# Experts' gate scale from maxima, routing weights on GpSimd, and a shifted order in a shared-and-routed MLP kernel

## What is computed

```python
def _gemma_mlp(x, gate_w, up_w, down_w):
    g = jnp.einsum('bsh,hi->bsi', x, gate_w)
    u = jnp.einsum('bsh,hi->bsi', x, up_w)
    return jnp.einsum('bsi,ih->bsh', gelu(g) * u, down_w)

rw = softmax(router_logits); w, sel = top_k(rw, 2); w = w / w.sum(-1)
dense_w = zeros((B, E)).at[arange(B)[:, None], sel].add(w)
out = sum over e of dense_w[:, e] * _gemma_mlp(x, skill_gate[e], skill_up[e], skill_down[e])
x = x + out + _gemma_mlp(x, shared_gate, shared_up, shared_down)
```

## Time and profile before

| | |
|---|---|
| median of 3 runs | 211.62 us (211.42 to 211.68) |
| the profiled execution | 211.93 us, its span 210.1 us |
| TensorE busy (2695 matmuls) | 205.2 us |
| VectorE busy | 123.6 us |
| ScalarE busy | 133.8 us |
| GpSimd busy | 117.9 us |
| granted TensorE clock | 1.0 all through |
| loads from HBM | 9.18 MB, landed in the first 26 us |

### The profile page before, as it was taken

One profiled execution on the slowest core, in us unless ns is written; L12 is line 12 of the kernel. 1 busy time (PEld: TensorE's weight loads), 2 busy tenths in 40 slices (PEclk: granted clock), 3 DMA queues, 4 the chain that ended last, 5 costly groups with the idle time before them and its releaser, 6 DMA issues.

```text
span 210.1 us, 6672 instructions
## 1 busy us (share of the span) xinstructions
PE 205.2 (98%) x2695; PEld 165.0 (79%) x2695; DVE 123.6 (59%) x217; ACT 133.8 (64%) x217; POOL 117.9 (56%) x129
## 2 busy tenths in 40 slices
PE   7999999989999999999999999999999999999995
PEld 2444555445444478899999999999999999999995
DVE  2899657977999988554353444434435435344452
ACT  6283767677989997655656656556565565655650
POOL 3023644359548997665565655655656556565562
PEclk9999999999999999999999999999999999999999
DMA  6999600000000000000010010010010010010011
GB/s 196 391 433 434 296 2 0 0 3 0 2 0 5 0 0 3 0 3 5 3 53 3 0 53 3 3 53 0 3 55 3 3 53 0 3 53 4 3 50 53
DMA packets 2813, 11.70 MB, mean 56 GB/s; under 512 B 352, under 2 KB 608, under 8 KB 2400
## 3 DMA queue, kind: packets, MB, share of 16 engines
q1 hardware_dynamic: 2640, 11.01, 13.1%
q10 hardware_dynamic: 144, 0.26, 0.7%
HBM read 9.18 MB, written 2.10 MB: 54 GB/s over the span
## 4 chain that ended last, share of the span: by engine, by line
PE 93%; DVE 4%; issue 1%; ACT 0%; POOL 0%; POOLq 0%
PE o_ps L664 7%; PE g_ps L646 7%; PE u_ps L646 7%; PE o_ps L663 7%; PE u_ps L645 7%; PE g_ps L645 7%; PE u_ps L644 7%; PE g_ps L644 7%; PE o_ps L662 7%; PE u_ps L612 3%; PE g_ps L612 3%; PE g_ps L614 2%; PE o_ps L627 2%; PE o_ps L625 2%; PE o_ps L626 2%; PE g_ps L613 2%
## 5 line engine op out<-in xcount | busy, mean ns | idle before, releaser
L304 POOL TENSOR_TENSOR h<-h 128x512 f16<-128x512 f32 x92 | 109.2, 1194 | 79.2 <-ACT h L340 57.9
L457 DVE SCALAR_TENSOR_TENSOR h<-gel,sk_factor,u_ps 128x512 f32<-128x512 f32 x64 | 47.8, 747 | 68.0 <-PE u_ps L646 39.0
L335 ACT ACTIVATE gel<-g_ps,sk_gate 128x512 f32<-128x512 f32 x64 | 43.9, 687 | 49.8 <-PE g_ps L646 49.8
L340 ACT CAST h<-h 128x512 f16<-128x512 f32 x92 | 56.0, 609 | 3.5 <-DVE h L457 3.5
L645 PE MATMUL g_ps<-x,wsk 128*128 128x128 f16 x256 | 46.2, 219 | 0.0
L646 PE MATMUL g_ps<-x,wsk 128*128 128x128 f16 x256 | 46.2, 219 | 0.0
L645 PE MATMUL u_ps<-x,wsk 128*128 128x128 f16 x256 | 46.2, 219 | 0.0
L646 PE MATMUL u_ps<-x,wsk 128*128 128x128 f16 x256 | 46.2, 219 | 0.0
L644 PE MATMUL u_ps<-x,wsk 128*128 128x128 f16 x256 | 46.2, 219 | 0.0
L644 PE MATMUL g_ps<-x,wsk 128*128 128x128 f16 x256 | 46.2, 219 | 0.0
L663 PE MATMUL o_ps<-h,wsk 128*128 128x128 f16 x256 | 45.9, 219 | 0.0
(11 more groups left out here) (103 smaller groups left out, 310.1 us busy)
## 6 DMA issues: line engine op xcount, KB each, us to landing
wsk<-skills SPq DMA_DIRECT2D x3, 2048.0 KB, 16.1
outT<-xT SPq DMA_DIRECT2D x7, 256.0 KB, 2.0
xT<-xT SPq DMA_DIRECT2D x2, 768.0 KB, 6.3
wsh<-shared SPq DMA_DIRECT2D x3, 256.0 KB, 3.9
xT<-xT ACTq DMA_DIRECT2D x1, 256.0 KB, 3.5
xT<-xT SPq DMA_DIRECT2D x1, 256.0 KB, 4.6
outT<-xT SPq DMA_DIRECT2D x1, 192.0 KB, 2.6
outT<-xT SPq DMA_DIRECT2D x1, 64.0 KB, 1.5
```

What stands on the lines that cost most here:

```text
L304: nc.gpsimd.tensor_tensor(hidden_lo(t), hidden_full(t), hidden_hi(t), ALU.subtract).then_inc(lo_ok, 1)
L335: nc.scalar.activation(gel[:, t % NG, :], g_ps[t % 2][:, :], ACT.Gelu_apprx_tanh, scale=scale).then_inc(gelu_ok, 1)
L340: nc.scalar.copy(hidden_hi(t), hidden_full(t)).then_inc(hi_ok, 1)
L457: nc.vector.scalar_tensor_tensor(out=h32[:, t % N32, :], in0=gel[:, t % NG, :], scalar=factor, in1=u_ps[t % 2][:, :], op0=ALU.mult, op1=AL ...
```

## The change

Four things change.

The experts' gate weights get their scale as x does: VectorE reduces them in steps 5 to 8, 1024 columns each (`part_top`), `mask` reduces the four maxima to one and squares it, and TensorE sums the square. The gram of the gate is gone from TensorE; GRAMS holds the two that stay.

The routing weights and their spreading move from VectorE at step 3 to GpSimd, behind `shared_tables(FIRST)` and in front of its first subtraction; one fused operation becomes two. The reciprocal moves on VectorE to the end of `probabilities`.

The low half of the shared down weights and `x_low(0)` move from behind `hidden(4)` to in front of it.

The hand-written order shifts: K_UP's gram begins at step 9 instead of 10, K_DOWN's at 16 instead of 15; the masks stand at 8, 11, 14, 20 (K_GATE, X_REST, K_UP, K_DOWN) and their sums at 10, 14, 17, 23; before, at 9, 12, 14, 19 and 11, 14, 16, 21. The last three x groups are reduced one step earlier, their high halves come one step later, the experts' pieces one step earlier, the tables of the experts two steps later.

```diff
-        TOP_AT = {1: (2,), 3: (3, 4), 10: (5,), 11: (6,), 12: (7,)}
-        TOP_OF = {FIRST: 3 + XF, X_NEXT: 3 + XA, X_REST: 3 + G}
-        K_STEPS = [5, 10, 15]
-        MASK_AT = {3: X_NEXT, 9: K_GATE, 12: X_REST, 14: K_UP, 19: K_DOWN}
-        SPREAD_AT = {4: X_NEXT, 11: K_GATE, 14: X_REST, 16: K_UP, 21: K_DOWN}
+        TOP_AT = {1: (2,), 3: (3, 4), 9: (5,), 10: (6,), 11: (7,)}
+        TOP_OF = {FIRST: 3 + XF, X_NEXT: 3 + XA, X_REST: 4 + G, K_GATE: 4 + XA}
+        PART_AT = {5: (GATE, 0), 6: (GATE, 1), 7: (GATE, 2), 8: (GATE, 3)}
+        K_STEPS = {K_UP: 9, K_DOWN: 16}
+        MASK_AT = {3: X_NEXT, 8: K_GATE, 11: X_REST, 14: K_UP, 20: K_DOWN}
+        SPREAD_AT = {4: X_NEXT, 10: K_GATE, 14: X_REST, 17: K_UP, 23: K_DOWN}
         ROUTE_AT = 6
-        ROUTED_AT = 11
+        ROUTED_AT = 10
-        SKILL_TABLES_AT = 23
-        X_AT = {3: 0, 5: 2, 8: 3, 11: 4, 15: 5, 19: 6, 23: 7}
+        SKILL_TABLES_AT = 25
+        X_AT = {3: 0, 5: 2, 8: 3, 12: 4, 16: 5, 20: 6, 24: 7}
-        PIECES = {12 + 2 * n: n for n in range(3 * E // EG)}
+        PIECES = {11 + 2 * n: n for n in range(3 * E // EG)}
...
+            def routing_weights():        # on GpSimd
+                pool.wait_ge(r_step, 6)
+                nc.gpsimd.tensor_copy(route[:, TOP_K:], top_i[:, 0:TOP_K])
+                nc.gpsimd.tensor_scalar(w_raw[:, :], top_v[:, 0:TOP_K], rpair[:, 0:1], None, ALU.mult).then_inc(r_weight, 1)
+                pool.wait_ge(r_weight, 1)
+                nc.gpsimd.tensor_scalar(w_live[:, :], w_raw[:, :], 1.0 / NUM_MOE_LAYERS, None, ALU.mult)
+                nc.gpsimd.tensor_scalar(w_rest[:, :], w_raw[:, :], 1.0 - 1.0 / NUM_MOE_LAYERS, None, ALU.mult).then_inc(r_weight, 1)
+                pool.wait_ge(r_weight, 2)
+                nc.gpsimd.tensor_tensor(route[:, 0:TOP_K], w_rest[:, :], w_live[:, :], ALU.add).then_inc(r_weight, 1)
+                pool.wait_ge(r_weight, 3)
+                for q in range(2 * TOP_K):
+                    nc.gpsimd.tensor_scalar(spread[:, :, q], ident[0:B, 0:B], route[:, q:q + 1], None, ALU.mult).then_inc(r_spread, 1)
...
+            def part_top(kind, n):
+                if n == 0:
+                    dve.wait_ge(sk_in[kind], 16)
+                nc.vector.tensor_reduce(parts[:, n:n + 1], wsk32[:, (kind * E + 2 * n) * I:(kind * E + 2 * n + 2) * I],
+                                        AX.X, ALU.max, apply_absolute_value=True).then_inc(part_ok, 1)
...
-                if n not in K_OF:
+                if n in K_OF and n not in GRAMS:
+                    kind = K_OF.index(n)
+                    dve.wait_ge(part_ok, E // 2)
+                    tops(KC + kind, parts[:, :])
+                if n not in GRAMS:
...
             for t in range(STEPS):
+                if t == C:
+                    shared_low(DOWN, 3)
+                    x_low(0)
                 hidden(t)
-                if t - 1 in X_AT:
+                if t - 1 in X_AT and t != C:
                     x_low(X_AT[t - 1])
...
+                if t in PART_AT:
+                    part_top(*PART_AT[t])
...
-                if t == C:
-                    shared_low(DOWN, 3)
...
-                if t == C - 1:
-                    routing_weights()
-                    routing_spread()
```

More of the change, by code:

```diff
@@ L73, in build @@
         ident = sb("ident", [P, P], F32)
+        parts = sb("parts", [P, E // 2], F32)
         floor = sb("floor", [P, 3 + XF], BF16)
@@ L108, in build @@
         w_raw = sb("w_raw", [B, TOP_K], F32)
+        w_rest = sb("w_rest", [B, TOP_K], F32)
         w_live = sb("w_live", [B, TOP_K], F32)
@@ L136, in build @@
         r_step = sem("r_step")
+        r_weight = sem("r_weight")
         r_spread = sem("r_spread")
@@ L141, in build @@
         top_ok = sem("top_ok")
+        part_ok = sem("part_ok")
         gram_ok = sem("gram_ok")
@@ L174, in build @@
         K_OF = (K_GATE, K_UP, K_DOWN)
+        GRAMS = (K_UP, K_DOWN)
         COLS = [(DC, XC + XF), (XC + XF, XC + XA), (KC, KC + 1), (XC + XA, XC + G), (KC + 1, KC + 2), (KC + 2, KC + 3)]
@@ L294, in skill_tables @@
                                         wexp[:, :, :].rearrange("p (j r) k -> p j (r k)", r=GR), ALU.mult).then_inc(tab_sk, 1)
+            def routing_weights():
[10 more added lines that the diff above has]
+                    nc.gpsimd.tensor_scalar(spread[:, :, q], ident[0:B, 0:B], route[:, q:q + 1], None, ALU.mult).then_inc(r_spread, 1)
             shared_tables(FIRST)
+            routing_weights()
             for t in range(C, STEPS):
@@ L394, in mask @@
                 else:
-                    kind = K_OF.index(n)
-                    dve.wait_ge(gram_ok, kind + 1)
+                    dve.wait_ge(gram_ok, GRAMS.index(n) + 1)
                     nc.vector.scalar_tensor_tensor(out=diag[:, :], in0=n_ps[0][:, 0:P], scalar=NORM_FLOOR,
@@ L403, in scales @@
                 norm = n_ps[1][:, 0:b - a]
-                if n in K_OF:
+                if n in GRAMS:
                     norm = n_all[:, a:b]
                     nc.vector.tensor_reduce(norm, n_ps[1][:, 0:P], AX.X, ALU.max).then_inc(n_red, 1)
-                    dve.wait_ge(n_red, K_OF.index(n) + 1)
+                    dve.wait_ge(n_red, GRAMS.index(n) + 1)
                 nc.vector.tensor_scalar(e_bits[:, a:b], norm.bitcast(U32), 1, EXP_MASK,
@@ L487, in probabilities @@
                 nc.vector.tensor_tensor(pair[:, :], top_v[:, 0:1], top_v[:, 1:2], ALU.add).then_inc(r_step, 1)
-            def routing_weights():
                 dve.wait_ge(r_step, 5)
-                nc.vector.tensor_copy(route[:, TOP_K:], top_i[:, 0:TOP_K]).then_inc(r_step, 1)
                 nc.vector.reciprocal(rpair[:, :], pair[:, :]).then_inc(r_step, 1)
[L493 to L504, removed]
             def routed_tables():
@@ L698, in _ @@
                     down_first(1)
-                for kind in range(3):
-                    n = t - K_STEPS[kind]
+                for batch in GRAMS:
+                    kind = K_OF.index(batch)
+                    n = t - K_STEPS[batch]
                     if 0 <= n < 4:
@@ L703, in _ @@
                             pe.wait_ge(sk_in[kind], 16)
-                        if n == 0 and kind:
-                            pe.wait_ge(diag_ok, K_OF[kind - 1] + 1)
+                        if n == 0 and batch == K_DOWN:
+                            pe.wait_ge(diag_ok, K_UP + 1)
                         a = (kind * E + 2 * n) * I
                         for half in range(2):
-                            last = gram(n_ps[0][:, 0:P], wsk32[:, a + half * I:a + (half + 1) * I],
-                                        n == 0 and half == 0)
+                            last = gram(n_ps[0][:, 0:P], wsk32[:, a + half * I:a + (half + 1) * I], n == 0 and half == 0)
                         if n == 3:
```

## The result

The changed kernel takes 209.61 us (median; 209.51 to 209.69) against 211.65 of the kernel before run beside it: a ratio of 0.9907 with a 95% interval of 0.9884 to 0.9930, 2.04 us less. On another chip the ratio was 0.9920 (0.9892 to 0.9949). The forecast was 209.8 us.

A forecast was written before the change was run, and what follows sets the result against it. TensorE was taken as the bound, with VectorE deciding only where its masks are late. Terms -1.84 - 0.49 - 1.01 + 0.5 + 0.68 + 0.35 = -1.81 us gave 209.8 us from the 211.62 median, range 208.5 to 211.3.

The forecast's parts named there:

- The products, -1.84: Steps 5 to 8: TensorE loses a row of eight 128-column products each, 0.46 us per row, 1.84 us saved.
- X_REST's mask, -0.49: Step 14's sum: the mask, moved to step 11, comes in time, so TensorE's 0.49 us wait goes whole.
- VectorE as pace of steps 5 to 11, +0.68: VectorE without a gap from hidden(5) delays x_low(3), so TensorE waits 0.68 us by step 8's down products.
- Two low halves: Before hidden(4): they fill the routing's place; X_NEXT's scales then escape GpSimd's 0.8 us hold-up, with no gain yet.
- The lock between VectorE and GpSimd at steps 2 and 3, +0.5: GpSimd's small routing operations slip between VectorE's two-input operations, delaying the X_NEXT sum 0 to 0.85 us; 0.5 taken.
- Rival B: Freed time turns into waits: VectorE-GpSimd lock 0.85, K_UP's mask late 0.8, reductions at 1.25; 211.0 us, chance 0.24.
- K_UP's mask, -1.01 + 0.35: K_DOWN gram: the 1.01 us wait goes; an even chance of a 0.7 us wait for the mask adds 0.35.
- A: New waits don't come: the lock costs nothing, reductions take 1.05 us, K_UP's mask is in time; 208.6 us, chance 0.18.
- C: VectorE's reductions become the bound and the kernel slower, from 1.7 us each; 212.4 us at 1.8, chance 0.08.

The follow-up runs named there:

- the maxima alone: Kernel before with only the experts' gate scaled from maxima (reductions in steps 5 to 8), routing and order unchanged: ratio 0.9984, stretch 65.53 us against 65.59.
- the long neighbours: Changed kernel plus two unused 128x512 GpSimd subtractions in front of the routing weights: 211.44 us, ratio 0.9989 to the kernel before.
- the mask in front: Changed kernel with step 14's mask of K_UP in front of the scales of X_REST instead of behind: ratio 0.9902 to the kernel before, stretch 63.44 us.

## Why the prediction was right, point by point

The total was right and three of its terms were not; that their errors cancel is luck.

*The products, -1.84.* Right: no gram stands in steps 5 to 8. K_UP's begins at 26.50 in the changed trace, which is 27.43 on the clock of the kernel before (the X_NEXT sum, 0.93 us later there, as the common point), against a forecast near 27.8. But the kernel with the maxima alone shows that this is what the change makes possible, not what it gains by itself.

*X_REST's mask, -0.49.* Right, the sum at 37.12 has no wait.

*VectorE as pace of steps 5 to 11, +0.68.* Right in its cause and place, measured 0.52 and 0.32, so 0.84. A reduction took 1.21 us, start to start 1.13, as it was put together from 512 columns:

```profile
L412 DVE TENSOR_REDUCE parts<-wsk x4: 1210/1212/1212, 19.4 to 26.0; 128x1 f32<-128x1024 f32 x4
```

The chain kept its time: hidden(5) began 0.59 us after its third up product (18.11 to 18.70) and not 0.48, the rest was shorter by as much, and x_low(3) came at 28.18, which is 29.11 on that clock, against 29.1. The missing 0.16 us lie behind it, on the way to TensorE:

```profile
29.07 1.16 POOL L324 TENSOR_TENSOR h<-h 128x512 f16<-128x512 f32 x1 [3.51 <-ACT h L360]
```

This subtraction ended at 30.23 and the down products began at 30.38, 0.15 us later, for which the sum had nothing (29.1, 0.89 and 1.14 make 31.13, too, and not 31.15). Halving the reductions took both waits away, which settles the cause.

*Two low halves.* Right: the scales of X_NEXT ended before GpSimd's first subtraction, and their second operation took 0.17 us (17.46) instead of 0.94.

*The lock between VectorE and GpSimd at steps 2 and 3, +0.5.* Wrong in size: 0.05 us in front of the X_NEXT sum before and after. The step took the hold-up that a whole subtraction causes, scaled to the 0.30 us span of a small GpSimd operation; the long neighbours show that the turn-taking is as it was read there (0.57 and 1.01 us), and the small ones that VectorE doesn't lose their spans. Rival B's first term falls with it. The Trainium skill's "SBUF — State Buffer", "Who interferes with whom", agrees with the long neighbours, each blocked until the other's end; what the prediction estimated from it for the small operations, 0.85 us, the trace doesn't show.

*K_UP's mask, -1.01 + 0.35.* Wrong in size. The step saw the very mechanism (the last scales operation beside the subtraction that skill_low(1) lets go), gave it an even chance and 0.7 us. It came, at 41.08, and the wait is 0.99: TensorE kept what it lost before. The kernel with the mask in front shows that this hold-up alone was enough for the wait. Most of the other 0.3 us come from the three earlier operations that meet a subtraction, which the sum had at 0.5 each: an x group's low half (37.24) and a pair of experts' (39.10) lost 0.53 each, and the last small operation of the routed tables 0.81:

```profile
31.74 0.97 DVE L529 CAST words<-words_f 1x8 int32<-1x8 f32 x1
```

In the kernel before it took 0.16, with no subtraction beside it. The prediction named a wait of over a microsecond in front of this gram as a sign of being wrong; it was 0.99, and 1.01 when the kernel was profiled again, so this part stands at that limit.

*What was left out.* The prediction read all else in the stretch as back to back. But two small waits of the kernel before went as well, 0.08 us in front of the K_UP gram and 0.10 us at step 24. So the trace's sum is -1.84 - 0.49 - 0.02 + 0.84 - 0.18 = -1.69, against 1.70 measured; the forecast's was -1.81 with the lock 0.5 too high, the masks 0.64 too low and the pace 0.16 too low, and 0.18 missing.

The timed difference, 2.04 us, has an interval from 1.5 to 2.5 us in which 1.70 lies; the second chip gave 1.7.

The rivals: A was right on the lock and fell on the waits that did come, 0.84 and 0.99 us. B fell on its lock term; its K_UP term came in full. C fell on the reductions, which kept their 1.21 us beside GpSimd.

## What to carry to other kernels

Moving work from a full engine to one with slack gains only as long as the second engine's queue keeps its due times: the maxima alone came to 0.06 us of their 1.84, and the change pays because room is made in that queue at the same time. Of what makes the room, the routing is worth 0.33 us here; what the masks' steps are worth wasn't measured. Look in the queue of the engine that takes the work over for the point from which it has no gap, and count from there to the operation that the bound engine waits for. What is taken out in front of that point gained little here (0.33 of 1.28 us for the routing); what is taken out behind it gained until the bound engine waited for something else (1.5 of 2.2 us for the halved reductions). And put what a bound engine waits for ahead of operations that a neighbour can hold up, however small they are.

## What the runs showed of the hardware

A VectorE operation on three columns can take 1.14 us beside a GpSimd subtraction. One column is not held: timelines of VectorE and GpSimd in the changed kernel, where the subtraction had begun 0.69 us before.

```profile
30.88 0.15 DVE L440 TENSOR_SCALAR i_bits<-e_bits 128x1 int32<-128x1 uint32 x1
```

```profile
30.19 1.16 POOL L324 TENSOR_TENSOR h<-h 128x512 f16<-128x512 f32 x1
```

In the fourteen traces of this case, 18 of the three-column operations at the end of `scales` began while a subtraction ran, and all 18 were held, to between 0.56 and 1.14 us; 50 of one column began so and none was (0.14 to 0.16 us). So the K batches' scales were free of the hold-up, and those of x were not. The cast of eight numbers shown above was held ten times of ten, the reductions of x and of the weights never in 31.

The first fp32 products ran at different rates in two executions. TensorE's timeline, the kernel before and the changed one, two passes each:

```profile
4.99 2.05 PE L594 MATMUL g_ps<-xT,wsh 128*128 128x512 f32 x2
```

```profile
4.86 1.10 PE L608 MATMUL g_ps<-xT,wsh 128*128 128x512 f32 x2
```

The granted clock reads 1.00 for this stretch in both, but the trace's record of the clock begins only at 7.04 us in the kernel before and at 4.61 in the changed one, so it says nothing of the slow products; their cause stays open. In the second profile of the changed kernel it was VectorE's wait of 1.26 us for x that made the first sum late. Over the fourteen traces that sum lies between 8.31 and 10.12 us, so two traces are best compared from a point behind the start.
